# Causal block: rows normalised sequence by sequence, both inverse roots from one variance

## The chip, the cores and the metric

One core of one Trainium2 chip. The time is the device time in microseconds (us) of one launch. Engines in the profile: PE is the tensor engine (TensorE), PEld its weight loads, DVE VectorE, ACT ScalarE, POOL GpSimd, SP the engine that starts DMAs.

## The reference, cut to what matters

The kernel computes a small language-model tower on 8 sequences of 1024 tokens with 64 channels: an embedding from a table, an attention block with 8 heads (called lattice here), and a block with causal attention and a mixture of 8 experts. The change lies in the causal attention. Its input is `h`; it is normalised twice before the projections:

```
x = layernorm(h)                      # (h - mean) / sqrt(var + 1e-5)
def _rmsnorm(v, w): return v * rsqrt(mean(v * v) + 1e-6) * w
h1 = _rmsnorm(x, ln1_w)
q, k, v = h1 @ wq.T, h1 @ wk.T, h1 @ wv.T      # 4 query heads, 2 key/value heads of 16
q = q * cos + rotate_half(q) * sin    # k in the same way
att = softmax(causal(q @ k.T / sqrt(16)))
x = x + (att @ v) @ wo.T
```

The mean square of the layer-normed row follows from the variance alone: with s2 the sum of squares of the centred row and v = s2/64 + 1e-5, the mean of x*x is (s2/64)/v.

## The kernel before

The launch runs four blocks one after the other: `embed`, `lattice`, `causal`, `experts`. All state stays in SBUF: `hres` holds the residual as 128 partitions by 64 rows by 64 channels, `x2` the layer-normed rows. A sequence (called batch, `b`) is 8 of the 64 rows (`TB = 8`), 512 elements on each partition.

`causal` begins with a prologue. GpSimd builds masks, SP loads weights, VectorE folds the norm's weights into them. Then VectorE and ScalarE normalise all 64 rows together (L947 to L968): sum, mean, centring into `x2` (L951), square on ScalarE (L885), sum of squares, variance, root on ScalarE (L887), reciprocal, scaling of `x2` (L960), and a second square, sum, root and reciprocal for the rms norm (`rinv`). Then batch 0 is prepared: `scale_tokens` (L974) makes `xs`, TensorE transposes it (L1046), ScalarE copies it out (L897), TensorE makes the four projections p0 to p3 and the values v (L1058, L1050), VectorE multiplies the projections with the cosine and sine tables (`table`, L984), GpSimd adds their halves and spreads q over the heads (`rope`: L854, L860, and L857 for k), ScalarE copies the values (L901).

The main part runs over batches in `over_batches`: body(0), a hardware loop whose pass holds two batches, then body(7) and a short body(8) that only finishes. A body has 32 units `n`, one for each of 8 blocks of 128 queries and 4 heads; the keys of a unit are 128 to 1024 wide and grow with n (a width for every four units). For unit n:

- TensorE makes the scores (L1084) in one of two score slots, transposes the probabilities of unit n-3 (L1104), and every four units multiplies with the values (L1131) for unit n-5; at n = 6 it applies `wo` (L1112).
- VectorE takes the masked maximum (L1000), copies transposed probabilities (L1014), and takes the reciprocal of the row sum (L1018). Units of VectorE are in this order in its queue.
- ScalarE takes the exponential with its sum (L914) and some of the copies (L924).
- GpSimd multiplies the probabilities with the reciprocal (L871).

The order of everything in a queue is written out by hand. Pieces for batch b+1 stand between the units of batch b: `PIECES` for TensorE (x at 9, p0 to p3 at 13 to 19, v at 21) and `ROPE` for GpSimd (q at 17, heads at 19 to 25, k at 27). At `ADD_AT = 7` VectorE adds the output of the batch before to `x2` (L1022) behind the reciprocal, and GpSimd adds `x2` to `hres` (L877).

`wait` waits on a semaphore, in the instruction that follows. `held`, and a wait with `nop(nofuse=True)` behind it, put the wait into an instruction of its own. In the trace a unit's number is found by counting the maxima (L1000): batch 1's unit 7 starts at 4815.73, unit 28 at 4869.56.

Of the kernel before, what the change touches and what calls it, by code (L numbers as in the profile page):

```python
# [6 lines left out]
ALU = mybir.AluOpType  # L7
ACT = mybir.ActivationFunctionType
AX = mybir.AxisListType.X
# [4 lines left out]
P = 128  # L14
B, S, D = 8, 1024, 64
NT = B * S // P
TB = S // P
# [13 lines left out]
def wait(eng, s, v):  # L31

    if not isinstance(v, int) or v > 0:
        eng.wait_ge(s, v)
# [678 lines left out]
def causal(nc, ident, hres, x2, wqk4, wvT, woT, ln1, cosT, sinT):  # L713

    with ExitStack() as ctx:
        def sb(name, shape, dt=F32):
            return ctx.enter_context(nc.sbuf_tensor(name, shape, dt))
# [1 line left out]
        UNITS = [(qt, h) for qt in range(TB) for h in range(NH)]  # L719
        NU = len(UNITS)  # L720

        sq = sb("c_sq", [P, NT, D])
        s1, mean, s2, var, std, rstd = (sb("c_" + n, [P, NT]) for n in ("s1", "mean", "s2", "var", "std", "rstd"))
        ms, rms, rinv = (sb("c_" + n, [P, NT]) for n in ("ms", "rms", "rinv"))
        lnw = sb("lnw1", [D, 1])
        wqk = sb("c_wqk", [D, 4, P])
        wv = sb("c_wv", [D, NKV * HD])
# [82 lines left out]
        def exists(b):  # L810
            return not isinstance(b, int) or 0 <= b < B

        def over_batches(eng, body):
            body(0, 0)
            with eng.Fori(1, B // 2) as i:
                body(2 * i - 1, 1)
                body(2 * i, 0)
            body(B - 1, (B - 1) % 2)
            body(B, B % 2)

        block = ctx.enter_context(nc.Block())

# [58 lines left out]

        @block.scalar
        def _(act):
            act.wait_ge(ln, 3)
            nc.scalar.activation(sq[:], x2[:], ACT.Square).then_inc(sqd, 1)  # L885
            act.wait_ge(ln, 5)
            nc.scalar.activation(std[:], var[:], ACT.Sqrt).then_inc(rooted, 1)  # L887
            act.wait_ge(ln, 7)
            nc.scalar.activation(sq[:], x2[:], ACT.Square).then_inc(sqd, 1)
            act.wait_ge(ln, 9)  # L890
            nc.scalar.activation(rms[:], ms[:], ACT.Sqrt).then_inc(rooted, 1)

            def tokens_out(b):
                wait(act, xT, b + 1)
# [10 lines left out]
            act.wait_ge(consts, 6)  # L905
            tokens_out(0)
            values_out(0, 0)

            def body(b, par):
                for n in range(steps(b)):  # L910
# [22 lines left out]
                        tokens_out(b + 1)  # L933
                    if pieces(b) and PIECES.get(n) == "v":
                        values_out(b + 1, 1 - par)
            over_batches(act, body)

        @block.vector
        def _(dve):
# [4 lines left out]
            nc.vector.tensor_scalar(wqk[:, 2:4], wqk[:, 2:4], lnw[:, 0:1], None, ALU.mult).then_inc(wmul, 1)  # L944
            nc.vector.tensor_scalar(wv[:], wv[:], lnw[:, 0:1], None, ALU.mult).then_inc(wmul, 1)

            nc.vector.tensor_reduce(s1[:], hres[:], AX, ALU.add).then_inc(ln, 1)  # L947
            dve.wait_ge(ln, 1)
            nc.vector.tensor_scalar(mean[:], s1[:], 1.0 / D, None, ALU.mult).then_inc(ln, 1)
            dve.wait_ge(ln, 2)  # L950
            nc.vector.tensor_tensor(x2[:], hres[:], mean[:].unsqueeze(2).to_broadcast([P, NT, D]),  # L951
                                    ALU.subtract).then_inc(ln, 1)
            dve.wait_ge(sqd, 1)
            nc.vector.tensor_reduce(s2[:], sq[:], AX, ALU.add).then_inc(ln, 1)
            dve.wait_ge(ln, 4)
            nc.vector.tensor_scalar(var[:], s2[:], 1.0 / D, EPS, ALU.mult, ALU.add).then_inc(ln, 1)
            dve.wait_ge(rooted, 1)
            nc.vector.reciprocal(rstd[:], std[:]).then_inc(ln, 1)
            dve.wait_ge(ln, 6)
            nc.vector.tensor_tensor(x2[:], x2[:], rstd[:].unsqueeze(2).to_broadcast([P, NT, D]),  # L960
                                    ALU.mult).then_inc(ln, 1)

            dve.wait_ge(sqd, 2)
            nc.vector.tensor_reduce(s2[:], sq[:], AX, ALU.add).then_inc(ln, 1)
            dve.wait_ge(ln, 8)
            nc.vector.tensor_scalar(ms[:], s2[:], 1.0 / D, EPS_RMS, ALU.mult, ALU.add).then_inc(ln, 1)
            dve.wait_ge(rooted, 2)
            nc.vector.reciprocal(rinv[:], rms[:]).then_inc(ln, 1)  # L968
            dve.wait_ge(ln, 10)

            def scale_tokens(b):

                wait(dve, xT, b)
                nc.vector.tensor_tensor(xs[:], x2[:, bass.ds(b * TB, TB), :],  # L974
                                        rinv[:, bass.ds(b * TB, TB)].unsqueeze(2).to_broadcast([P, TB, D]),
                                        ALU.mult).then_inc(scaled, 1)

            def table(b, par, i):
# [4 lines left out]
                wait(dve, roped, b)  # L983
                nc.vector.tensor_tensor(dst, sc[:, SLOT["p%d" % i]], tab[:], ALU.mult).then_inc(done, 1)  # L984

            scale_tokens(0)
            for i in range(4):
                table(0, 0, i)

            dve.wait_ge(consts, 6)  # L990

            def body(b, par):
                for n in range(steps(b)):
# [22 lines left out]
                    if exists(b):  # L1016
                        wait(dve, expd, NU * b + n + 1)
                        nc.vector.reciprocal(rs[:, par, n:n + 1], sm[:, par, n:n + 1]).then_inc(recip, 1)  # L1018
                    if n == ADD_AT and exists(b - 1):
                        wait(dve, wd, b)  # L1020
                        xv = x2[:, bass.ds((b - 1) * TB, TB), :]
                        nc.vector.tensor_tensor(xv, yp[:].rearrange("p (t d) -> p t d", d=D), xv,  # L1022
                                                ALU.add).then_inc(w_sb, 1)
# [579 lines left out]
```

## Time and profile before

| what | us |
|---|---|
| median of 3 runs (5791.23 to 5793.92) | 5791.73 |
| the profiled execution, its own time | 5820.83 |
| its span | 5819.0 |
| start of the causal prologue's normalising (L947) | 4679.13 |
| first maximum of batch 0 | 4734.01 |
| last addition of the stage (L877) | 5351.86 |

The profiled execution is one of its own and a little longer than the runs that give the median. Times of rows are microseconds from the span's start. The causal stage is about a tenth of the span; `lattice` takes most of the rest, and the change doesn't touch it.

### The profile page before, as it was taken

To read this page: it belongs to the slowest core of one execution; us is meant where nothing else is said; L and a number is where in the kernel's file an instruction comes from. 1 tells how busy PE (TensorE), PEld (TensorE's weight loads), DVE (VectorE), ACT (ScalarE), POOL (GpSimd) and SP (SyncE) were. 2 spreads that over 40 slices of the span, in tenths; PEclk is the share of its full clock that TensorE was granted. 3 is DMA by queue.
4 is the path that set the end of the run, shared out by engine and by line. 5 is a ranking of instruction groups with operands and counts; after the bars stand their busy time and mean duration, and the time that the engine had idled before them with its cause. 6 is when DMAs were issued, how large, how long until landed. Compare 5 with 4: busy or idle time off the path is not lost. (4 is left out here: it accounts for less than half of the span.)

```text
span 5819.0 us, 98405 instructions
## 1 busy us (share of the span) xinstructions
PE 4780.6 (82%) x27646; PEld 2687.0 (46%) x27689; DVE 4160.0 (71%) x7651; ACT 3990.3 (69%) x5494; POOL 3775.7 (65%) x3599
## 2 busy tenths in 40 slices
PE   2788888888888888888888888888888869996999
PEld 1344444444444444444444444444444436554666
DVE  3677777777777777777777777777777656666665
ACT  1677777777777777777777777777777734444332
POOL 4677777777777777777777777777777634443233
PEclk8899999999999999999999999999999879998999
DMA  1000000000000000000000000000000000000000
GB/s 20 9 8 9 8 10 8 8 8 8 8 8 8 8 8 8 9 8 10 8 8 8 8 8 8 8 8 8 9 8 10 3 9 2 2 2 15 3 6 8
DMA packets 34205, 45.42 MB, mean 8 GB/s; under 512 B 24521, under 2 KB 24585, under 8 KB 34058
## 3 DMA queue, kind: packets, MB, share of 16 engines
q1 hardware_dynamic: 32010, 43.49, 2.8%
q0 software_dynamic: 2048, 0.14, 0.1%
q8 instruction: 72, 1.18, 0.1%
q14 instruction: 75, 0.61, 0.0%
HBM read 39.40 MB, written 4.19 MB: 7 GB/s over the span
## 5 line engine op out<-in xcount | busy, mean ns | idle before, releaser
L617 PE MATMUL banks<-ident,att 128*128 128x128 f32 x8192 | 1145.5, 287 | 408.6 <-DVE ag L549 247.1
L617 PEld LDWEIGHTS banks<-ident,att 128*128 128x128 f32 x8192 | 940.7, 147 | 1003.0 <-DVE ag L549 617.4
L659 PE MATMUL banks<-kT,qT 128*128 128x512 f32 x2048 | 1144.1, 658 | 275.8 <-DVE mx L578 266.5
L419 POOL TENSOR_TENSOR sinb<-sinb,ag 128x1024 f32<-128x1024 f32 x512 | 1280.7, 2505 | 82.7 <-ACT sinb L490 68.9
L569 DVE SCALAR_TENSOR_TENSOR mag<-near,mag 128x512 f32<-128x512 int32 x1024 | 859.6, 844 | 479.3 <-POOL near L435 470.6
L429 POOL TENSOR_SCALAR mag<-mag 128x512 f32<-128x512 f32 x1024 | 689.2, 677 | 567.7 <-DVE mag L569 533.7
L676 PE MATMUL outp<-work,vo 128*64 128x512 f32 x2048 | 1043.4, 634 | 0.0
L676 PE MATMUL outp<-sinb,vo 128*64 128x512 f32 x2048 | 1043.4, 634 | 0.0
L435 POOL TENSOR_SCALAR near<-mag 128x512 int32<-128x512 f32 x1024 | 796.4, 778 | 354.2 <-ACT mag L508 291.5
L508 ACT ACTIVATE mag<-banks 128x512 f32<-128x512 f32 x1024 | 598.7, 592 | 278.0 <-PE banks L659 276.4
L526 DVE TENSOR_TENSOR work<-banks,work 128x1024 f32<-128x1024 f32 x512 | 625.3, 1221 | 190.3 <-ACT work L484 187.7
L484 ACT ACTIVATE work<-banks,halfpi 128x1024 f32<-128x1024 f32 x512 | 571.2, 1116 | 239.8 <-PE banks L617 232.8
L490 ACT ACTIVATE sinb<-banks 128x1024 f32<-128x1024 f32 x512 | 522.8, 1021 | 247.7 <-PE banks L633 247.7
L424 POOL TENSOR_SCALAR att<-att,rs 128x1024 f32<-128x1024 f32 x384 | 543.7, 1416 | 214.8 <-DVE rs L543 188.0
L549 DVE TENSOR_TENSOR ag<-banks,work 128x1024 f32<-128x1024 f32 x512 | 621.0, 1213 | 73.3 <-ACT work L513 73.0
L501 ACT ACTIVATE work<-banks 128x1024 f32<-128x1024 f32 x512 | 522.1, 1020 | 155.4 <-PE banks L617 149.0
L659 PEld LDWEIGHTS banks<-kT,qT 128*128 128x128 f32 x2048 | 346.9, 204 | 609.6 <-DVE mx L578 395.1
L472 ACT ACTIVATE att<-att,nb 128x1024 f32<-128x1024 f32 x512 | 582.0, 1139 | 0.8
L513 ACT ACTIVATE work<-work 128x1024 f32<-128x1024 f32 x512 | 541.8, 1058 | 8.3
L676 PEld LDWEIGHTS outp<-work,vo 128*64 128x64 f32 x2048 | 248.0, 141 | 568.9 <-issue 555.6
L578 DVE CUSTOM_DVE_ANT_0 att<-mag,banks 128x512 f32<-128x512 f32 x512 | 348.2, 680 | 211.6 <-POOL mag L429 211.5
L563 DVE TENSOR_SCALAR nturn<-att 128x1024 bf16<-128x1024 f32 x512 | 417.4, 825 | 85.1 <-POOL att L424 85.1
(198 smaller groups left out, 6362.8 us busy)
## 6 DMA issues: line engine op xcount, KB each, us to landing
x<-xT_dram SPq DMA_DIRECT2D x128, 256.0 KB, 3.5
xT_dram<-xT SPq DMA_DIRECT2D x8, 256.0 KB
out<-hres SPq DMA_DIRECT2D x8, 256.0 KB, 2.6
base<-in_L_tok_turns,idx POOLq DMA_INDIRECT x64
wqk<-in_L_attn_Wq SPq DMA_DIRECT2D x64, 16.0 KB
wqk<-in_L_attn_Wk SPq DMA_DIRECT2D x64, 16.0 KB
wqk<-in_L_attn_bq SPq DMA_DIRECT2D x64, 0.2 KB
wqk<-in_L_attn_bk SPq DMA_DIRECT2D x64, 0.2 KB
```

The lines of the kernel that those rows point to most:

```text
L419: nc.gpsimd.tensor_tensor(sinb[:, k % RING], sinb[:, k % RING], ag[:, k], ALU.mult).then_inc(tmul, 1)
L429: nc.gpsimd.tensor_scalar(mag[:, n % 4], mag[:, n % 4], 1.0, PHI, ALU.mult, ALU.add).then_inc(factor, 1)
L435: nc.gpsimd.tensor_scalar(near[:, n % 4], mag[:, n % 4], 1.0 / 6.0, 1.0, ALU.add, ALU.mult).then_inc(rounded, 1)
L472: nc.scalar.activation(att[:, p, j], att[:, p, j], ACT.Exp, bias=nb[:, p, j:j + 1], scale=EXPSCALE, accum_out=ssum[:, j:j + 1]).then_inc(e ...
L484: nc.scalar.activation(pair(work[:, k % RING]), turn_pair(k), ACT.Sin, bias=halfpi[:, 0:1], scale=-C2 / TURN).then_inc(cosd, 1)
L508: nc.scalar.activation(mag[:, n % 4], score_bank(n), ACT.Abs).then_inc(mags, 1)
L526: nc.vector.tensor_tensor(pair(work[:, k % RING]), turn_pair(k), pair(work[:, k % RING]), ALU.mult).then_inc(acd, 1)
L549: nc.vector.tensor_tensor(pair(ag[:, d]), turn_pair(d), pair(work[:, d % RING]), ALU.mult).then_inc(agd, 1)
L569: nc.vector.scalar_tensor_tensor(mag[:, n % 4], near[:, n % 4], 1.0, mag[:, n % 4], ALU.mult, ALU.is_gt).then_inc(kept, 1)
L617: mm = nc.tensor.matmul(turn_pair(k)[:, c, i * P:(i + 1) * P], att[:, p, 4 * half + i, kt * P:(kt + 1) * P], ident[:], is_transpose=True, ...
L659: nc.tensor.matmul(score_bank(n), qT[:, p, (n // 2) * P:(n // 2 + 1) * P], kT[:, p, (n % 2) * 512:(n % 2 + 1) * 512], start=True, stop=Tru ...
L676: mm = nc.tensor.matmul(outp[rows], vo[:, kt, :], term[:, k % RING, c * 512:(c + 1) * 512], start=(kt == 0), stop=(kt == TB - 1), skip_gro ...
```

## The change

Rows are now normalised by sequence. The prologue does the whole chain for batch 0, then batch 1 (its sum and centring before the `table` multiplications of batch 0, the rest behind them). Batch b+2 is normalised between the units of batch b: VectorE does sum and mean after the reciprocal of unit 22, the centring after that of 24, the second moments after 27, the scaling after 30; ScalarE does the square after unit 25 and the root after unit 28. The second mean square is worked out from the first (`rv`, `prod`), so there is one square and one root, over 16 columns, for both norms. Each wait in these parts has a nop of its own. The hardware loop ends one pass earlier, and batches 5 and 6 are written out as 7 and 8 are.

```
--- before.py
+++ after.py
@@ -719,9 +719,10 @@
         UNITS = [(qt, h) for qt in range(TB) for h in range(NH)]
         NU = len(UNITS)
 
-        sq = sb("c_sq", [P, NT, D])
-        s1, mean, s2, var, std, rstd = (sb("c_" + n, [P, NT]) for n in ("s1", "mean", "s2", "var", "std", "rstd"))
-        ms, rms, rinv = (sb("c_" + n, [P, NT]) for n in ("ms", "rms", "rinv"))
+        sq = sb("c_sq", [P, TB, D])
+        s1, mean, s2, rv, prod = (sb("c_" + n, [P, TB]) for n in ("s1", "mean", "s2", "rv", "prod"))
+        moments, root = (sb("c_" + n, [P, 2, TB]) for n in ("moments", "root"))
+        inverse = sb("c_inverse", [P, 2, TB])
         lnw = sb("lnw1", [D, 1])
         wqk = sb("c_wqk", [D, 4, P])
         wv = sb("c_wv", [D, NKV * HD])
@@ -810,13 +811,18 @@
         def exists(b):
             return not isinstance(b, int) or 0 <= b < B
 
+        SUM_AT, CENTRE_AT, SQUARE_AT, MOMENTS_AT, ROOT_AT, SCALE_AT = 22, 24, 25, 27, 28, 30
+
+        def normalised(b):
+            return not isinstance(b, int) or b + 2 < B
+
         def over_batches(eng, body):
             body(0, 0)
-            with eng.Fori(1, B // 2) as i:
+            with eng.Fori(1, B // 2 - 1) as i:
                 body(2 * i - 1, 1)
                 body(2 * i, 0)
-            body(B - 1, (B - 1) % 2)
-            body(B, B % 2)
+            for b in range(B - 3, B + 1):
+                body(b, b % 2)
 
         block = ctx.enter_context(nc.Block())
 
@@ -881,14 +887,18 @@
 
         @block.scalar
         def _(act):
-            act.wait_ge(ln, 3)
-            nc.scalar.activation(sq[:], x2[:], ACT.Square).then_inc(sqd, 1)
-            act.wait_ge(ln, 5)
-            nc.scalar.activation(std[:], var[:], ACT.Sqrt).then_inc(rooted, 1)
-            act.wait_ge(ln, 7)
-            nc.scalar.activation(sq[:], x2[:], ACT.Square).then_inc(sqd, 1)
-            act.wait_ge(ln, 9)
-            nc.scalar.activation(rms[:], ms[:], ACT.Sqrt).then_inc(rooted, 1)
+            def squares(b):
+                wait(act, ln, 10 * b + 3)
+                act.nop(nofuse=True)
+                nc.scalar.activation(sq[:], x2[:, bass.ds(b * TB, TB), :], ACT.Square).then_inc(sqd, 1)
+
+            def roots(b):
+                wait(act, ln, 10 * b + 8)
+                act.nop(nofuse=True)
+                nc.scalar.activation(root[:], moments[:], ACT.Sqrt).then_inc(rooted, 1)
+
+            squares(0)
+            roots(0)
 
             def tokens_out(b):
                 wait(act, xT, b + 1)
@@ -905,6 +915,8 @@
             act.wait_ge(consts, 6)
             tokens_out(0)
             values_out(0, 0)
+            squares(1)
+            roots(1)
 
             def body(b, par):
                 for n in range(steps(b)):
@@ -933,6 +945,10 @@
                         tokens_out(b + 1)
                     if pieces(b) and PIECES.get(n) == "v":
                         values_out(b + 1, 1 - par)
+                    if normalised(b) and n == SQUARE_AT:
+                        squares(b + 2)
+                    if normalised(b) and n == ROOT_AT:
+                        roots(b + 2)
             over_batches(act, body)
 
         @block.vector
@@ -944,35 +960,50 @@
             nc.vector.tensor_scalar(wqk[:, 2:4], wqk[:, 2:4], lnw[:, 0:1], None, ALU.mult).then_inc(wmul, 1)
             nc.vector.tensor_scalar(wv[:], wv[:], lnw[:, 0:1], None, ALU.mult).then_inc(wmul, 1)
 
-            nc.vector.tensor_reduce(s1[:], hres[:], AX, ALU.add).then_inc(ln, 1)
-            dve.wait_ge(ln, 1)
-            nc.vector.tensor_scalar(mean[:], s1[:], 1.0 / D, None, ALU.mult).then_inc(ln, 1)
-            dve.wait_ge(ln, 2)
-            nc.vector.tensor_tensor(x2[:], hres[:], mean[:].unsqueeze(2).to_broadcast([P, NT, D]),
-                                    ALU.subtract).then_inc(ln, 1)
-            dve.wait_ge(sqd, 1)
-            nc.vector.tensor_reduce(s2[:], sq[:], AX, ALU.add).then_inc(ln, 1)
-            dve.wait_ge(ln, 4)
-            nc.vector.tensor_scalar(var[:], s2[:], 1.0 / D, EPS, ALU.mult, ALU.add).then_inc(ln, 1)
-            dve.wait_ge(rooted, 1)
-            nc.vector.reciprocal(rstd[:], std[:]).then_inc(ln, 1)
-            dve.wait_ge(ln, 6)
-            nc.vector.tensor_tensor(x2[:], x2[:], rstd[:].unsqueeze(2).to_broadcast([P, NT, D]),
-                                    ALU.mult).then_inc(ln, 1)
-
-            dve.wait_ge(sqd, 2)
-            nc.vector.tensor_reduce(s2[:], sq[:], AX, ALU.add).then_inc(ln, 1)
-            dve.wait_ge(ln, 8)
-            nc.vector.tensor_scalar(ms[:], s2[:], 1.0 / D, EPS_RMS, ALU.mult, ALU.add).then_inc(ln, 1)
-            dve.wait_ge(rooted, 2)
-            nc.vector.reciprocal(rinv[:], rms[:]).then_inc(ln, 1)
-            dve.wait_ge(ln, 10)
+            def reached(b, k):
+                wait(dve, ln, 10 * b + k)
+                dve.nop(nofuse=True)
+
+            def rows(x, b):
+                return x[:, bass.ds(b * TB, TB), :]
+
+            def wide(x):
+                return x.unsqueeze(2).to_broadcast([P, TB, D])
+
+            def sums(b):
+                nc.vector.tensor_reduce(s1[:], rows(hres, b), AX, ALU.add).then_inc(ln, 1)
+                reached(b, 1)
+                nc.vector.tensor_scalar(mean[:], s1[:], 1.0 / D, None, ALU.mult).then_inc(ln, 1)
+
+            def centre(b):
+                reached(b, 2)
+                nc.vector.tensor_tensor(rows(x2, b), rows(hres, b), wide(mean[:]), ALU.subtract).then_inc(ln, 1)
+
+            def second_moments(b):
+                wait(dve, sqd, b + 1)
+                dve.nop(nofuse=True)
+                nc.vector.tensor_reduce(s2[:], sq[:], AX, ALU.add).then_inc(ln, 1)
+                reached(b, 4)
+                nc.vector.tensor_scalar(moments[:, 0], s2[:], 1.0 / D, EPS, ALU.mult, ALU.add).then_inc(ln, 1)
+                reached(b, 5)
+                nc.vector.reciprocal(rv[:], moments[:, 0]).then_inc(ln, 1)
+                reached(b, 6)
+                nc.vector.tensor_tensor(prod[:], s2[:], rv[:], ALU.mult).then_inc(ln, 1)
+                reached(b, 7)
+                nc.vector.tensor_scalar(moments[:, 1], prod[:], 1.0 / D, EPS_RMS, ALU.mult, ALU.add).then_inc(ln, 1)
+
+            def scale_rows(b):
+                wait(dve, rooted, b + 1)
+                dve.nop(nofuse=True)
+                nc.vector.reciprocal(inverse[:], root[:]).then_inc(ln, 1)
+                reached(b, 9)
+                nc.vector.tensor_tensor(rows(x2, b), rows(x2, b), wide(inverse[:, 0]), ALU.mult).then_inc(ln, 1)
 
             def scale_tokens(b):
 
                 wait(dve, xT, b)
-                nc.vector.tensor_tensor(xs[:], x2[:, bass.ds(b * TB, TB), :],
-                                        rinv[:, bass.ds(b * TB, TB)].unsqueeze(2).to_broadcast([P, TB, D]),
+                reached(b, 10)
+                nc.vector.tensor_tensor(xs[:], rows(x2, b), wide(inverse[:, 1]),
                                         ALU.mult).then_inc(scaled, 1)
 
             def table(b, par, i):
@@ -983,9 +1014,20 @@
                 wait(dve, roped, b)
                 nc.vector.tensor_tensor(dst, sc[:, SLOT["p%d" % i]], tab[:], ALU.mult).then_inc(done, 1)
 
+            def whole(b):
+                sums(b)
+                centre(b)
+                second_moments(b)
+                scale_rows(b)
+
+            whole(0)
             scale_tokens(0)
+            sums(1)
+            centre(1)
             for i in range(4):
                 table(0, 0, i)
+            second_moments(1)
+            scale_rows(1)
 
             dve.wait_ge(consts, 6)
 
@@ -1016,6 +1058,15 @@
                     if exists(b):
                         wait(dve, expd, NU * b + n + 1)
                         nc.vector.reciprocal(rs[:, par, n:n + 1], sm[:, par, n:n + 1]).then_inc(recip, 1)
+                    if normalised(b):
+                        if n == SUM_AT:
+                            sums(b + 2)
+                        if n == CENTRE_AT:
+                            centre(b + 2)
+                        if n == MOMENTS_AT:
+                            second_moments(b + 2)
+                        if n == SCALE_AT:
+                            scale_rows(b + 2)
                     if n == ADD_AT and exists(b - 1):
                         wait(dve, wd, b)
                         xv = x2[:, bass.ds((b - 1) * TB, TB), :]
```

## Rows read from the trace of the kernel before

**Rows 1.** Page, first part: busy us, share of the span, instructions of each engine.
```profile
PE 4780.6 (82%) x27646; PEld 2687.0 (46%) x27689; DVE 4160.0 (71%) x7651; ACT 3990.3 (69%) x5494; POOL 3775.7 (65%) x3599
```

**Rows 2.** Busy times by window: one batch, and the stretch with the low clock.
```profile
4817.00:4895.00 78.00, 73.10 (x584) 47.11 (x584) 51.49 (x136) 36.60 (x84) 34.58 (x40) 0.98 0.01 2
4819.00:4824.00 5.00, 4.26 (x17) 3.11 (x17) 2.37 (x9) 1.85 (x4) 1.37 (x3) 0.66 0.01 3
```

**Rows 3.** Timeline of VectorE, start of the causal stage.
```profile
4679.13 4.41 DVE L947 TENSOR_REDUCE c_s<-hres 128x64 f32<-128x4096 f32 x1
...
4711.12 0.69 DVE L974 TENSOR_TENSOR c_xs<-x,c_rinv 128x512 f32<-128x512 f32 x1
...
4734.01 0.29 DVE L1000 CUSTOM_DVE_ANT_0 c_pr<-c_sc,c_mask 128x128 f32<-128x128 f32 x1 [3.54 <-PE c_sc L1084]
```

**Rows 4.** Timeline of ScalarE, the same stretch.
```profile
4691.89 1.28 ACT L887 ACT_TABLE_LOAD   x1
...
4732.49 0.38 ACT L901 ACTIVATE c_v<-c_sc 128x256 f32<-128x256 f32 x1 [17.43 <-PE c_sc L1050]
```

**Rows 5.** Timeline of VectorE, last batch of the embedding stage.
```profile
125.74 0.69 DVE L189 TENSOR_REDUCE s<-hres 128x8 f32<-128x512 f32 x1
126.46 0.17 DVE L191 TENSOR_SCALAR mean<-s 128x8 f32<-128x8 f32 x1
...
129.69 0.69 DVE L208 TENSOR_TENSOR xn<-cen,rstd 128x512 f32<-128x512 f32 x1
```

**Rows 6.** Timeline of ScalarE, an exponential among the experts.
```profile
5421.45 1.28 ACT L1274 ACT_TABLE_LOAD   x1
5422.74 0.26 ACT L1274 ACTIVATE e_prob<-e_prob 128x64 f32<-128x64 f32 x1
```

**Rows 7.** Timeline of VectorE, units 7 and 8 of batches 0 and 1.
```profile
4741.70 0.42 DVE L1000 CUSTOM_DVE_ANT_0 c_pr<-c_sc,c_mask 128x256 f32<-128x256 f32 x1
...
4742.95 0.56 DVE L1000 CUSTOM_DVE_ANT_0 c_pr<-c_sc,c_mask 128x384 f32<-128x384 f32 x1
...
4815.73 0.42 DVE L1000 CUSTOM_DVE_ANT_0 c_pr<-c_sc,c_mask 128x256 f32<-128x256 f32 x1 [0.21 <-PE c_sc L1084]
...
4817.56 0.55 DVE L1000 CUSTOM_DVE_ANT_0 c_pr<-c_sc,c_mask 128x384 f32<-128x384 f32 x1
...
4818.03 1.72 DVE L974 TENSOR_TENSOR c_xs<-x,c_rinv 128x512 f32 x1
```

**Rows 8.** Timeline of GpSimd: its additions of two tensors, batch 1.
```profile
4817.93 1.27 POOL L877 TENSOR_TENSOR hres<-hres,x  x1 [0.30 <-DVE x L1022]
...
4870.63 2.38 POOL L857 TENSOR_TENSOR c_k<-c_k,c_ks 128x1024 f32<-128x1024 f32 x1
```

**Rows 9.** Timeline, units 25 to 29 of batch 1: VectorE, and TensorE's scores for unit 29.
```profile
4861.89 1.09 DVE L1000 CUSTOM_DVE_ANT_0 c_pr<-c_sc,c_mask 128x896 f32<-128x896 f32 x1 [0.47 <-PE c_sc L1084]
...
4869.33 0.17 DVE L1018 RECIPROCAL c_rs<-c_sm 128x1 f32<-128x1 f32 x1 [0.73 <-ACT c_pr L914]
4869.56 1.22 DVE L1000 CUSTOM_DVE_ANT_0 c_pr<-c_sc,c_mask 128x1024 f32<-128x1024 f32 x1
...
4871.82 1.98 PE L1084 MATMUL c_sc<-c_k,c_qh 128*128 128x512 f32 x4
...
4874.03 1.23 DVE L1000 CUSTOM_DVE_ANT_0 c_pr<-c_sc,c_mask 128x1024 f32<-128x1024 f32 x1 [1.76 <-PE c_sc L1084]
```

**Rows 10.** Timeline of ScalarE, the exponential of unit 29.
```profile
4875.30 1.15 ACT L914 ACTIVATE c_pr<-c_pr,c_nm 128x1024 f32<-128x1024 f32 x1 [2.86 <-DVE c_nm L1000]
```

**Rows 11.** Timeline: unit 1 of batch 2, then units 0 and 1 of batch 3.
```profile
4884.46 0.29 DVE L1000 CUSTOM_DVE_ANT_0 c_pr<-c_sc,c_mask 128x128 f32<-128x128 f32 x1 [0.44 <-PE c_sc L1084]
...
4960.24 0.77 PE L1084 MATMUL c_sc<-c_k,c_qh 128*128 128x128 f32 x2 [3.70 <-issue]
...
4961.35 0.29 DVE L1000 CUSTOM_DVE_ANT_0 c_pr<-c_sc,c_mask 128x128 f32<-128x128 f32 x1 [3.09 <-PE c_sc L1084]
...
4965.38 0.29 DVE L1000 CUSTOM_DVE_ANT_0 c_pr<-c_sc,c_mask 128x128 f32<-128x128 f32 x1 [1.87 <-PE c_sc L1084]
```

## Prediction

> **What bounds the kernel now.** I read the page's first part first: the tensor engine (TensorE) is busy for 82% of the span, VectorE for 71%, ScalarE for 69%, and no DMA queue matters [rows 1]. That says nothing yet of the causal stage, which is a tenth of the span, so I then read the busy times of one of its batches: 78 us with TensorE busy for 73.1, VectorE for 51.5, ScalarE for 36.6 and GpSimd for 34.6 [rows 2]. It looks like a stage that TensorE bounds. The timeline says otherwise. In a unit the order is: VectorE takes the maximum (L1000), ScalarE the exponential (L914), VectorE the reciprocal (L1018), then the next maximum. Maximum and reciprocal sit on one engine with the exponential between them, so a unit can't be shorter than their sum. The reciprocal of unit 27 starts at 4869.33 and the maximum of unit 28 at 4869.56 [rows 9]; nothing else lies between them. TensorE's scores are mostly ready. What VectorE does between a maximum and its reciprocal is hidden behind the exponential; what it does after a reciprocal and ahead of the next maximum is not. The change puts all its new VectorE work in the second place.
>
> A test of this lies in the trace. The addition L1022 (512 columns, as the operations of 0.69 us in [rows 5]) stands after the reciprocal of unit 7, in every batch but the first. Without it the maxima of units 7 and 8 start 1.25 us apart (4741.70, 4742.95), with it 1.83 us (4815.73, 4817.56): 0.58 us of 0.69 comes through [rows 7]. So although TensorE is busy for 94% of the batch, VectorE's work at this place costs nearly its full length.
>
> **The prologue.** All 64 rows are now normalised before any token is scaled: from 4679.13 (L947) to 4711.12 (L974) is 32.0 us, and nothing else runs but these two engines [rows 3]. After the change only eight rows stand there. The embedding stage does almost the same chain on eight rows: from its sum at 125.74 to its scaling at 129.69, 0.69 long, is 4.64 us, each short operation taking 0.17 to 0.2 and starting 0.04 after its predecessor [rows 5]. The new chain has three more short operations (reciprocal of the variance, product, second moment), 3 × 0.21 = 0.6. Its waits are held by a nop of their own. What such a wait costs is seen at unit 29: the scores end at 4871.82 + 1.98 = 4873.80 and the maximum starts at 4874.03, 0.23 later instead of 0.04 [rows 9]. With 11 such links at some 0.17 more, 1.9 us. The table for the root was loaded in the shade of L954 (1.28 us at 4691.89) [rows 4]; now the nop carries the wait and the load stands between nop and root, so I take it as exposed. Bounds: 0 if the load is ahead of the nop, 1.28 if behind; I take 1.28. Sum 4.64 + 0.6 + 1.9 + 1.3 = 8.4, so 23.6 us are saved (bounds 23.6 to 26.8, the latter with neither nops nor load).
>
> Batch 1 is normalised in the prologue too. Its sum and centring fall into VectorE's wait for the first projections, free. Its second half can't: the square stands in ScalarE's queue behind the copy of the values, which starts at 4732.49 and lasts 0.38 [rows 4]. From 4732.9: square 0.6, reduce 0.7, four short operations 0.7, root 0.2, reciprocal 0.2, scale 0.7, and eight links at 0.2 make 4.7, which ends at 4737.6. The first maximum was at 4734.01 [rows 3] and stands behind it: +3.6 us (2.4 with links at 0.04). GpSimd's k rotation, which by the same time runs in batch 0, is over before the product.
>
> **The loop, six batches (b = 0 to 5).** Four blocks on VectorE and two on ScalarE:
> - Sums, after the reciprocal of unit 22: reduce 0.69, link 0.2, mean 0.17, and 0.1 for the register address: 1.2 us.
> - Centring, after unit 24: 0.69 + 0.2 = 0.9. Unit 25's maximum waits 0.47 for TensorE [rows 9], whose order doesn't depend on what was delayed, and that is absorbed: sum so far 1.6.
> - The square on ScalarE after unit 25: about 0.6, in ScalarE's idle time while VectorE takes the next maximum. 0; if that cover were gone, 0.6.
> - Second moments, after unit 27: 0.1 + 0.68, then four short operations of 0.17 to 0.2 and four links of 0.2: 2.3. But the product reads two SBUF tensors, and GpSimd starts its own two-tensor addition L857 at 4870.63, 1.1 us after the reciprocal, for 2.38 us [rows 8]. What happens then is seen in L974: it starts at 4818.03, GpSimd's addition L877 runs from 4817.93 to 4819.20, and the 0.69 us operation takes 1.72 and ends 0.55 after it [rows 7, 8]. So the product is held until L857 ends, 3.5 us after the reciprocal, and the block lasts 3.9. Bounds 2.3 and 3.9, I take 3.9, as the address pattern and the engines are those of the row. Unit 29's maximum waits 1.76 for TensorE [rows 9] and absorbs that much: 2.1 remain.
> - The root, after unit 28's exponential on ScalarE. The table of Exp is resident, so each batch has two loads, root's and back. In the experts stage a load takes 1.28, and the next activation starts 1.29 after the load [rows 6]. Two loads and the root (at most 0.26) are 2.85 with their gaps. ScalarE idled 2.86 ahead of unit 29's exponential [rows 10], but 1.76 of that was TensorE's wait, used up above; 1.1 hide, 1.75 come through. If the moments take 2.3 only, some 1.2 come through.
> - Scaling, after unit 30: 0.1 + reciprocal 0.2 + link 0.3 + 0.69 = 1.3, no two-tensor GpSimd work beside it.
>
> A batch costs 1.6 + 2.1 + 1.75 + 1.3 = 6.75 us, six cost 40.5. Without the hold on the product it is 1.6 + 0.5 + 1.2 + 1.3 = 4.6, six 27.6.
>
> The Trainium skill's page ScalarE: Activation LUTs (What ACT_TABLE_LOAD costs) has 1283 ns for the load and about 1380 ns of drain, 2.66 us a switch. The load agrees; the drain isn't in the rows. By the page, 12 switches would cost 12 × 1.37 = 16.4 us more.
>
> **The loop's edge.** The change also unrolls two batches more, so the loop is passed twice instead of three times and turns back once instead of twice. A turn costs: TensorE sits 3.70 for issue, VectorE idles 3.09 ahead of unit 0 and 1.87 ahead of unit 1, where 0.44 is usual [rows 11]. One turn less is −4.5 us. Unrolled batches have constants for registers; I take nothing for that (at most 1 us in all). The nop ahead of each scaling of tokens (seven) adds about 0.1 each behind no cover: +0.7, and SP issues nothing new.
>
> **Sum.** −23.6 + 3.6 + 40.5 − 4.5 + 0.7 = +16.7 us. The profiled execution took 5820.83, its span 5819.0; it would take 5837.5. The runs' median lies 29 below the profiled time, and no part of this is in the causal stage that I can see, so I add to the median: 5791.7 + 16.7 = 5808.4.
>
> **The rivals.** Changes within 0.2%, 11.6 us, are what a measurement of this kernel can't tell from none.
> - *The product isn't held (chance 0.2).* An eight-column operation may slip between the other engine's reads; no row shows so small a one beside L857. For it: TensorE is idle for only 5 us of 78, so a delay is soaked up more easily than I let it. Then −23.6 + 3.6 + 27.6 − 4.5 + 0.7 = +3.8: 5795.5.
> - *Faster (0.13): TensorE is the bound after all.* 94% busy speaks for it, unit 7 against. TensorE would catch up a delay of units 22 to 31 in the narrow units 0 to 8 of the next batch, where VectorE waits for it again and again. Then each batch gives back all but 2 us: −23.8 + 12 = −12: 5779.9. It decides below 2.1 us a batch.
> - *TensorE's clock (0.17).* At 4819 to 4824 the granted clock was 0.66 of full, a mixture of 2.4 and 1.2 GHz, after TensorE had idled for about a microsecond, and its matmuls were slower [rows 2]. It happened in one batch of six at that place. Idle stretches of some 4 us at units 28 to 30 could bring it in every batch: I take 2 us each, from the 1.87 − 0.44 = 1.4 that follows the loop's turn and up. +12: 5820.4.
> - *The table switch costs its drain (0.05)*: 1.37 us exposed twelve times, as worked out above: 5825.
> - My own case has the rest, 0.45, with 5802 to 5813.
>
> **Numbers.** 5808.4; range 5784 to 5824, which leaves out most of the faster case and the end of the dearest. Faster by over 0.2% (below 5780.1): 0.1. Within it: the first rival, half of the faster one and a sixth of mine: 0.34. Slower (above 5803.3): 0.56.
>
> **What the profile after would show.** L974's first instruction some 8.4 us after the first sum, not 32. The first maximum of batch 0 3.6 us later behind the projections than now. Product's duration about 1.8 us and not 0.17 in each of the six batches, ending as L857 ends. Two loads of 1.28 a batch around the root, and the exponential of unit 29 late by them. Six batches longer by some 6.8 us from unit 22 to the next unit 0. One idle stretch of 3.7 us of TensorE for issue in place of two. I am wrong if TensorE's idle time doesn't grow by what VectorE's does, if units 0 to 8 get shorter after a late unit 31, or if the load comes ahead of the nop.

## The result

| | before | changed |
|---|---|---|
| median of 13 runs each, us | 5791.88 | 5814.66 |
| ratio, 95% interval | | 1.0035 [1.0026, 1.0043] |
| span of the profiled execution, us | 5819.0 | 5810.4 |
| start of attention's last addition (L538) to the first maximum, us | 63.7 | 41.5 |
| first to last maximum, us | 605.3 | 649.3 |
| the whole stage, from that start to the start of the last addition to `x2`, us | 680.7 | 702.5 |

The change makes the kernel slower by 0.35%, some 20 us (15 to 25). The two spans seem to say the opposite, but the profiled execution of before had lost time ahead of the stage: its attention block starts (L398) at 136.7 and that of the changed kernel at 105.8. Inside the causal stage the traces differ by 702.5 − 680.7 = 21.8 us, which fits the measured 20. I therefore compare stages, not spans, from here on. In the changed kernel VectorE's maximum is L1042, its reciprocal L1060, the exponential L926, the scores L1135, GpSimd's multiplication L877 and its k rotation L863.

The prologue of the changed kernel, VectorE (answers to [rows 3]):

```profile
4649.67 0.67 DVE L974 TENSOR_REDUCE c_s<-hres 128x8 f32<-128x512 f32 x1
4650.44 0.17 DVE L976 TENSOR_SCALAR c_mean<-c_s 128x8 f32<-128x8 f32 x1
...
4656.90 0.69 DVE L1006 TENSOR_TENSOR c_xs<-x,c_inverse 128x512 f32<-128x512 f32 x1
...
4679.27 0.69 DVE L985 TENSOR_REDUCE c_s<-c_sq 128x8 f32<-128x512 f32 x1 [3.03 <-ACT c_sq L893]
...
4682.46 0.28 DVE L1042 CUSTOM_DVE_ANT_0 c_pr<-c_sc,c_mask 128x128 f32<-128x128 f32 x1
```

and ScalarE in the same stretch (to [rows 4]):

```profile
4654.13 1.28 ACT L898 ACT_TABLE_LOAD   x1 [2.00 <-DVE c_moments L993]
...
4678.26 0.38 ACT L911 ACTIVATE c_v<-c_sc 128x256 f32<-128x256 f32 x1 [17.42 <-PE c_sc L1101]
4678.54 0.62 ACT L893 ACTIVATE c_sq<-x 128x512 f32<-128x512 f32 x1
```

From the first sum to the scaling of tokens it is 7.2 us instead of 32.0. The load stands behind the wait for the moments, exposed. From there to the first maximum it is 25.6 instead of 22.9, because batch 1's second half waits for a square that stands behind the copy of the values.

Units 27 to 31 of batch 1 in the changed kernel, VectorE (to [rows 9]):

```profile
4827.70 0.16 DVE L1060 RECIPROCAL c_rs<-c_sm 128x1 f32<-128x1 f32 x1 [0.73 <-ACT c_pr L926]
4827.87 0.69 DVE L985 TENSOR_REDUCE c_s<-c_sq 128x8 f32<-128x512 f32 x1
4828.66 0.41 DVE L987 TENSOR_SCALAR c_moments<-c_s 128x8 f32<-128x8 f32 x1
4829.17 0.20 DVE L989 RECIPROCAL c_rv<-c_moments 128x8 f32<-128x8 f32 x1
4829.48 1.92 DVE L991 TENSOR_TENSOR c_prod<-c_s,c_rv 128x8 f32<-128x8 f32 x1
4831.50 0.17 DVE L993 TENSOR_SCALAR c_moments<-c_prod 128x8 f32<-128x8 f32 x1
4831.75 1.22 DVE L1042 CUSTOM_DVE_ANT_0 c_pr<-c_sc,c_mask 128x1024 f32<-128x1024 f32 x1
...
4834.58 1.22 DVE L1042 CUSTOM_DVE_ANT_0 c_pr<-c_sc,c_mask 128x1024 f32<-128x1024 f32 x1
...
4841.52 0.16 DVE L1060 RECIPROCAL c_rs<-c_sm 128x1 f32<-128x1 f32 x1 [0.84 <-ACT c_pr L926]
4841.60 0.25 DVE L998 RECIPROCAL c_inverse<-c_root 128x16 f32<-128x16 f32 x1
4841.96 1.55 DVE L1000 TENSOR_TENSOR x<-x,c_inverse 128x512 f32 x1
4843.43 1.21 DVE L1042 CUSTOM_DVE_ANT_0 c_pr<-c_sc,c_mask 128x1024 f32<-128x1024 f32 x1
...
4846.26 0.29 DVE L1042 CUSTOM_DVE_ANT_0 c_pr<-c_sc,c_mask 128x128 f32<-128x128 f32 x1
...
4849.90 0.29 DVE L1042 CUSTOM_DVE_ANT_0 c_pr<-c_sc,c_mask 128x128 f32<-128x128 f32 x1 [2.06 <-PE c_sc L1135]
```

GpSimd beside it (to [rows 8]):

```profile
4829.01 2.36 POOL L863 TENSOR_TENSOR c_k<-c_k,c_ks 128x1024 f32<-128x1024 f32 x1
...
4841.85 1.12 POOL L877 TENSOR_SCALAR c_pr<-c_pr,c_rs 128x1024 f32<-128x1024 f32 x1 [1.66 <-DVE c_rs L1060]
```

ScalarE at unit 29 (to [rows 6, 10]):

```profile
4834.65 1.28 ACT L898 ACT_TABLE_LOAD   x1
4835.94 0.22 ACT L898 ACTIVATE c_root<-c_moments 128x16 f32<-128x16 f32 x1
4836.17 1.28 ACT L926 ACT_TABLE_LOAD   x1
4837.47 1.15 ACT L926 ACTIVATE c_pr<-c_pr,c_nm 128x1024 f32<-128x1024 f32 x1
```

and two groups of TensorE's transposes, between the scores of unit 31 and those of unit 0 of batch 2:

```profile
4838.64 0.60 PE L1155 MATMUL c_pt<-ident,c_pr 128*128 128x128 f32 x4
4842.11 1.09 PE L1155 MATMUL c_pt<-ident,c_pr 128*128 128x128 f32 x4 [2.88 <-ACT c_prT L936]
```

The product of eight columns takes 1.92 us and ends with GpSimd's addition (4829.01 + 2.36 = 4831.37). The wide scaling takes 1.55 and ends 0.54 after GpSimd's L877, which has one tensor only. Two loads and a root stand in a row ahead of the exponential. TensorE then waits 2.88 us for a copy, and its next four transposes take 1.09 where four took 0.60.

The granted clock in the 6 us from unit 0 of batch 2, the changed kernel (busy times of the engines, then the clock, as in [rows 2]):

```profile
4846.00:4852.00 6.00, 5.90 (x81) 4.98 (x80) 3.37 (x13) 2.25 (x8) 1.86 (x3) 0.76 0.02 4
```

and the kernel before at the same place:

```profile
4882.00:4888.00 6.00, 5.86 (x108) 5.02 (x110) 4.37 (x18) 3.62 (x13) 2.24 (x4) 1.00 0.02 4
```

In the kernel before the clock is 1.00 at the start of batches 1, 2, 4 and 6, and 0.79 at that of 3 and 5, where the loop has just turned. In the changed kernel it is 0.65 to 0.82 at the start of all six. Such a window catches only the end of the slow stretch: ahead of batch 2 of the changed kernel the clock is 0.50 from 4842, as TensorE comes out of its wait of 2.88 us, to 4849, and unit 0 starts at 4846.26. Unit 31 lies in this stretch and costs nothing more (2.83 us, 2.85 before); unit 0 does.

Laid side by side by the starts of the maxima, batch 1 (unit 0: the start of batch 2), us from one unit's maximum to the next:

| unit | 22 | 24 | 27 | 28 | 29 | 30 | 0 |
|---|---|---|---|---|---|---|---|
| before | 2.36 | 2.93 | 2.54 | 4.47 | 2.78 | 2.78 | 2.02 |
| changed | 3.68 | 3.16 | 6.35 | 2.83 | 4.40 | 4.45 | 3.64 |
| difference | +1.3 | +0.2 | +3.8 | −1.6 | +1.6 | +1.7 | +1.6 |

Over all batches the 44.0 us between first and last maximum are: units 22 to 30 +39.3, unit 0 +5.9, unit 9 +3.2, unit 31 −3.4 (the loop's turn), the rest −1.0.

### The profile page after: what moved, and what is told of

It reads as the page before. It is cut to its first block and busy times, and to the rows that moved or that the text cites. A ratio compares the mean times of both kernels' runs of the same rounds, so it can differ in the third digit from the quotient of the medians.

```text
span 5810.4 us, 98228 instructions
## 1 busy us (share of the span) xinstructions
PE 4804.7 (83%) x27689; PEld 2704.4 (47%) x27689; DVE 4185.2 (72%) x7721; ACT 4004.3 (69%) x5518; POOL 3777.1 (65%) x3599
```

## The experiments

They ran on other chips, on which the kernel before took 5855 to 5860 us (medians) and scattered more; the ratio is always to runs of before on the same chip. An effect of 10 us (0.17%) doesn't show in such times, but it does in the stage of one trace, whose units 22 to 30 repeat from run to run within some 0.02 us where nothing was done to them. Units 0 and 9 don't: the clock decides their length, and they carry up to 3 us from one trace to another.

**Move GpSimd's k rotation.**

```
-        ROPE = {17: "q", 19: 0, 21: 1, 23: 2, 25: 3, 27: "k"}
+        ROPE = {17: "q", 19: 0, 21: 1, 23: 2, 25: 3, 28: "k"}
```

> The changed kernel with one number changed: GpSimd's k rotation stands behind unit 28 instead of 27, so it no longer runs beside the second moments. Theory (the product of eight columns is held by the two-tensor addition, 1.6 us a batch): the product takes 0.17 us in the loop instead of 1.91, the interval from the maximum of unit 27 to that of 28 falls from 6.35 to about 4.7, the sum of the causal stage (first to last maximum, 649.3 us) falls by 6 x 1.6 = 10, the time is some 10 us below the changed kernel's 5812. Rival (TensorE sets the pace there, or the operation is slow for another reason): the product gets short and unit 28 or 29 gives the time back, or it stays at 1.9; the sum stays at 649.

Ratio 1.0006 [0.9959, 1.0052]: the time says nothing. The stage is 690.8 us, 11.7 less than the changed kernel's 702.5. The interval of unit 27 fell from 6.35 to 4.60, that of 29 stayed at 4.39 and 30 at 4.45. The product for batch 2, worked out in batch 0:

```profile
4786.38 0.17 DVE L991 TENSOR_TENSOR c_prod<-c_s,c_rv 128x8 f32<-128x8 f32 x1
```

So the product was held by that one addition, 1.75 us a batch (10.4 of the 11.7; the rest is unit 9's), and nothing gives it back. One of its batches also shows that the slow stretch moves about: ahead of batch 3, where the loop turns, TensorE waits 2.79 us as ahead of batch 2, the clock is 0.50 from 4965 to 4972, and unit 0, which starts at 4972.09, takes 1.84 us at 1.00.

**No table switch in the loop.** A copy replaces the root of batches 2 to 7, so the root is left out there.

```
+                func = ACT.Sqrt if isinstance(b, int) and b < 2 else ACT.Copy
-                nc.scalar.activation(root[:], moments[:], ACT.Sqrt).then_inc(rooted, 1)
+                nc.scalar.activation(root[:], moments[:], func).then_inc(rooted, 1)
```

> The changed kernel with a copy in place of the root in batches 2 to 7, so that ScalarE keeps its table (what is computed is no longer the normalisation there). Theory (two table loads of 1.28 us, 1.6 us of them exposed at unit 29): the interval from the maximum of unit 29 to that of 30 falls from 4.40 to about 2.8, the stage by 6 x 1.6 = 10 us or more, since TensorE also idles less and its clock may stay up at the next unit 0. Rival (the page's 2.66 us for each switch): 4.3 us a batch, 26 in all. Second rival (TensorE's or GpSimd's lateness lies behind the loads): less than 3 us in all.

Ratio 1.0008 [0.9963, 1.0052]. The stage is 692.3 us, 10.3 less. Unit 29 fell from 4.40 to 2.78 and no other unit between 22 and 30 moved. Two switches a batch cost 1.62 us, not the rival's 4.3; but unit 0 stayed at about 3.6, so the clock was not won back.

**Both edits** (the root is left out here too).

> Both edits of the two runs before together: the k rotation behind unit 28 and no table switch in the loop. The question is the granted clock at the start of the next batch. In the changed kernel it is 0.65 to 0.82 in the 6 us from unit 0, where the kernel before has 1.00 unless the loop has just turned, and the interval from unit 0 to unit 1 is 1.4 to 2.0 us longer. Theory (the clock falls because TensorE has idled at units 28 to 31): with both stalls gone the clock is 1.00 there, unit 0 back at 2.0 us, and the two together save more than the sum of the two alone: 2 x 10 + 6 x 1.6 = 30 us, about 5783. Rival (unit 0 is late because TensorE has work left over, or the fall comes from elsewhere): the savings just add, 20 us, about 5792.

Ratio 1.001 [0.9964, 1.0057], stage 685.2: 17.3 less, not 30 and not even the 22 that the two add up to. Units 27, 29 are at 4.60 and 2.78. But unit 0 is no better: 3.49 to 4.28 us in five batches of six (2.88 behind the loop's turn). The window from unit 0 of batch 2, columns as before:

```profile
4916.00:4922.00 6.00, 5.98 (x68) 5.10 (x69) 2.05 (x8) 2.03 (x8) 1.50 (x2) 0.50 0.01 3
```

My expectation failed: the clock is 0.50, that is 1.2 GHz, for the whole window. It didn't fall lower than in the changed kernel, but later. Here the 0.50 lasts from 4915 to 4922, and unit 0 starts at 4916.88, so most of it falls on units 0 and 1. What was left was the stall behind unit 30. TensorE's transposes ahead of unit 0 came behind a wait of 1.96 us:

```profile
4916.02 1.09 PE L1156 MATMUL c_pt<-ident,c_pr 128*128 128x128 f32 x4 [1.96 <-DVE c_prT L1057]
```

**Both edits, and the scaling ahead of unit 30's reciprocal.**

```
+                    if normalised(b) and n == SCALE_AT:
+                        scale_rows(b + 2)
                     if exists(b):
                         wait(dve, expd, NU * b + n + 1)
                         nc.vector.reciprocal(rs[:, par, n:n + 1], ...)
...
-                        if n == SCALE_AT:
-                            scale_rows(b + 2)
```

> The run with both edits (k rotation behind unit 28, no table switch) and the scaling of unit 30 put ahead of the reciprocal. With both edits TensorE's clock still fell at the next unit 0 (3.5 to 4.3 us from unit 0 to 1, 2.0 in the kernel before); what was left there was the scaling, 1.7 us between units 30 and 31. Theory (that stall is what the clock falls after): unit 30's interval about 3.3 or less, unit 0's back at 2.0, clock 1.00 in the 6 us from unit 0. Rival (the stall at unit 27, or something of the units 28 to 31 as a whole): unit 0 stays at 3.5 or more.

One execution, 5827.6 us, so there is no ratio; the stage is 663.0, 22.2 less than with both edits alone. Unit 30 is at 2.78 as in the kernel before: the scaling has vanished under the exponential. Unit 0 is at 1.87 to 2.17, but for the loop's turn (3.75). The same window, and the same transposes:

```profile
4886.00:4892.00 6.00, 5.90 (x102) 5.03 (x104) 4.28 (x17) 3.70 (x13) 2.25 (x4) 1.00 0.02 4
```

```profile
4885.83 0.63 PE L1156 MATMUL c_pt<-ident,c_pr 128*128 128x128 f32 x4 [0.30 <-DVE c_prT L1057]
```

So with the other two gone, one stall of 1.7 us at unit 30 cost 22.2 / 6 = 3.7 us a batch: itself (10.2 of the 22.2 are unit 30's), and about as much again in slow matmuls (10.9 in units 0 and 1, 1.0 in unit 9).

**The scaling alone moved ahead**, held product and table loads in place; the diff is the one above, made to the changed kernel.

> The changed kernel with the scaling of unit 30 alone put ahead of the reciprocal; the held product and the table loads stay. Theory (TensorE's clock falls at unit 0 behind the scaling's stall, whatever came before): unit 30's interval 4.45 to 2.8 and unit 0's 3.2 to 4.0 back to about 2.0, 3.5 us a batch, the stage 702.5 to about 681. Rival (the clock falls after the sum of stalls from unit 27 on, so that with product and tables still there it falls anyway): unit 0 stays at 3.5, the stage at 692.

Ratio 1.0008 [0.9989, 1.0027], stage 688.5, 14.0 less. Of these 10.2 are unit 30's, and 3.0 unit 9's, which was slow in one batch instead of three for a reason that isn't known; without these 3.0 the stage would be at 691.5, near the rival's figure. Unit 30 is at 2.78, unit 0 at 2.9 to 3.4 outside the loop's turn, which is 0.9 to 1.4 above what it was before, and 5.04 behind the turn (4.03 before). The theory failed: the fall isn't tied to the scaling alone. TensorE's wait of 2.88 us at unit 30 is still there, and the fall comes behind it. This wait belongs to the table loads: it is 2.79 us with the rotation moved and 1.2 without the loads. Unit 0 does get shorter outside the turn (3.9, 3.6, 3.4, 4.0 and 3.5 were 3.1, 3.0, 2.9, 3.0 and 3.4).

**All four blocks ahead of the reciprocals.**

```
                     if exists(b):
-                        wait(dve, expd, NU * b + n + 1)
-                        nc.vector.reciprocal(...)                      # unit n
                     if normalised(b):
                         if n == SUM_AT:
                             sums(b + 2)
...
+                    if exists(b):
+                        wait(dve, expd, NU * b + n + 1)
+                        nc.vector.reciprocal(...)
```

> The changed kernel with VectorE's four blocks ahead of the reciprocals of units 22, 24, 27 and 30 instead of behind them, where they run while ScalarE takes the exponential. Theory (a unit is maximum, exponential, reciprocal in series, so only the place behind the reciprocal costs its full length): most of the blocks is covered, 0.5 to 0.9 us each; the product is also done before GpSimd's k rotation starts, since that waits for this reciprocal. The intervals fall at 22 from 3.68 to about 3.1, at 27 from 6.35 to about 3.6, at 30 from 4.45 to about 3.3; unit 29 stays at 4.4 (the tables). The sum from first to last maximum falls from 649.3 to some 625. Rival (VectorE's total or TensorE bounds the units, the place makes no odds): it stays within 3 us of 649.

Ratio 0.9967 [0.995, 0.9983]: faster than before. The stage is 660.4 us, 42.1 less than the changed kernel's, and the sum between first and last maximum 606.8; I had expected 625. Units 22 and 27 are at 2.97 and 3.41, 24 at 2.93, 28 at 3.60 (up from 2.83), 29 at 3.63, 30 at 2.78, and unit 0 at 1.87 to 2.19 but for the loop's turn. TensorE's longest wait at units 27 to 31, the turn aside, is 1.6 us, and its clock stays at 1.00. The moments of batch 2, VectorE:

```profile
4783.22 0.17 DVE L991 TENSOR_TENSOR c_prod<-c_s,c_rv 128x8 f32<-128x8 f32 x1
4783.49 0.17 DVE L993 TENSOR_SCALAR c_moments<-c_prod 128x8 f32<-128x8 f32 x1
4783.57 0.15 DVE L1069 RECIPROCAL c_rs<-c_sm 128x1 f32<-128x1 f32 x1
```

GpSimd's k rotation starts at 4784.87 there, after the product: in GpSimd's queue it stands behind L877, which waits for this reciprocal. My expectation was 18 us too small. The clock, which I had left out, makes 7.7 of them at unit 0; unit 30 gave 3.3 more than expected, because the scaling was covered in full, units 22, 24 and 27 gave 1 each, and unit 9 1.6. Against the kernel before, units 22 to 30 are 6.5 us a batch longer in one place, with a slow start of the next batch, and 1.0 us in the other.

**The loop alone.**

```
-            with eng.Fori(1, B // 2) as i:
+            with eng.Fori(1, B // 2 - 1) as i:
                 body(2 * i - 1, 1)
                 body(2 * i, 0)
-            body(B - 1, (B - 1) % 2)
-            body(B, B % 2)
+            for b in range(B - 3, B + 1):
+                body(b, b % 2)
```

> The kernel before with only the loop changed: one pass fewer, batches 5 and 6 written out. Theory (a turn of the loop costs 3.7 us of issue on TensorE and a fallen clock behind it, 4.95 us by the maxima of units 31 and 0): 5 us less, 5787, the stage 605.3 to about 600. Rival (written-out batches cost instruction fetches of their own): no change or slower.

Ratio 0.9982 [0.9933, 1.0031], which can't tell 5 us from none; stage 675.4, 5.3 less. One stretch of units 31 and 0 went from 5.9 + 3.9 to 2.9 + 2.0.

**Both roots from one variance, alone**: as in the changed kernel, but over all 64 rows in the prologue of the kernel before.

> The kernel before with one part of the change alone: all 64 rows still normalised in the prologue, but both roots from one variance (one square, one sum of squares and one root fewer, three short operations more). Theory: a square of 3.6 us and a reduction of 4.4 go, some 1 us comes; the first maximum is 8 us earlier (63.7 to about 55.7 us from the end of the attention block), everything behind it as before: 8 us less. Rival: nothing, because the projections or the weights are what the prologue waits for; the first maximum stays at 63.7.

Ratio 0.9988 [0.9972, 1.0004], which takes in both 7 us and none. In the trace the first maximum comes at 56.6 us instead of 63.7 (counted as in the table above), where 55.7 was expected, and from first to last maximum it is 605.1 as before: 7.1 us less. This half of the change was good.

**The rows in the gaps of the prologue.** The other seven batches, in pieces of 24 and 32 rows:

```
+            sums(0)
+            centre(0)
+            second_moments(0)
+            scale_rows(0)
             dve.wait_ge(w_in, 144)
...
             scale_tokens(0)
+            sums(1)
+            centre(1)
+            sums(2)
             table(0, 0, 0)
+            centre(2)
             table(0, 0, 1)
+            second_moments(1)
             table(0, 0, 2)
+            second_moments(2)
             table(0, 0, 3)
+            scale_rows(1)
+            scale_rows(2)
```

> A version built on the theory: batch 0 is normalised while VectorE waits for the weights (7.4 us idle in the kernel before), the other seven batches in two pieces in the gaps of VectorE between the projections of batch 0, nothing in the units; loop one pass shorter. Theory (the prologue's gaps are free, the units' are not): first maximum 63.7 - 32 + 3 to 6 = 35 to 38 us after the end of the attention block, the sum from first to last maximum 599.8 as with the short loop alone, the whole stage 680.7 to about 649, some 32 us (0.55%) faster than before. Rival (the pieces are held by GpSimd's rotation or push the projections back): first maximum at 45 or later, 20 us or less.

Ratio 0.9944 [0.9923, 0.9965]. First maximum at 38.9, a little later than expected, from first to last 598.2, stage 648.8, 31.9 less than before. VectorE in the gaps:

```profile
4701.05 0.35 DVE L988 TENSOR_SCALAR c_wqk<-c_wqk,lnw 64x256 f32<-64x256 f32 x1 [1.05 <-DMA c_wo<-in_woT]
...
4718.08 1.07 DVE L972 TENSOR_SCALAR c_moments<-c_prod 128x24 f32<-128x24 f32 x1
...
4725.02 3.71 DVE L980 TENSOR_TENSOR x<-x,c_inverse 128x1536 f32<-128x1536 f32 x1
...
4729.23 2.29 DVE L980 TENSOR_TENSOR x<-x,c_inverse 128x2048 f32<-128x2048 f32 x1
```

and GpSimd:

```profile
4716.90 4.41 POOL L862 TENSOR_SCALAR c_qh<-c_q,c_own 128x1024 f32<-128x1024 f32 x4 [0.18 <-POOL c_q L856]
4724.78 2.34 POOL L859 TENSOR_TENSOR c_k<-c_k,c_ks 128x1024 f32<-128x1024 f32 x1 [3.48 <-DVE c_ks L1008]
```

The weights are now waited for 1.05 us instead of 7.4. The row of the kernel before:

```profile
4678.45 0.34 DVE L942 TENSOR_SCALAR c_wqk<-c_wqk,lnw 64x256 f32<-64x256 f32 x1 [7.41 <-DMA c_wo<-in_woT]
```

The scaling of 24 rows is held by the k rotation (3.71 us, fewer elements than the 2.29 us behind it).

**The same, all batches written out, no loop.**

```
+            for b in range(B + 1):
+                body(b, b % 2)
```

> The version with the pieces in the projections' gaps, and all batches written out, no loop. Theory (a turn of the loop costs 4.9 us, written-out instructions are fetched in time): the interval from unit 31 of batch 2 to unit 0 falls from 5.81 to about 3.0 and the next from 4.21 to 2.2, the stage 648.8 to about 643, 38 us (0.65%) faster than before. Rival (instruction fetches fall behind when nothing is looped): stalls for issue on TensorE at other places, the stage at 649 or above.

Ratio 0.9921 [0.9896, 0.9946], the fastest version run. Stage 640.4, 40.3 less than before and 8.4 less than with the loop: 5.2 in units 31 and 0, the rest spread over the other units of the batches that had been in the loop. The batches between the first and the last last 75.1 us each, where those of the loop took 76 to 79, and the clock at unit 0 is 1.00 in all of them. No wait of TensorE for issue replaces the loop's turn.

## Why the prediction was right

The time, 5791.9 × 1.0035 = 5812, lies 4 above the forecast of 5808.4 (the median of the 13 runs 6 above), in the range and on the side foreseen. The mechanism was mine; several terms were off, and one rival was true as well. That the sum came so near is partly luck: it left out up to 11.1 us of lower clock, and 4.8 us of terms that were too dear stood against them.

- *Prologue*: −23.6 was forecast, 32.0 − 7.2 = 24.8 saved. The load is exposed as supposed; a held wait costs about 0.10 here (4649.67 + 0.67 to 4650.44), not 0.2, so the saving was put too small. For the same reason batch 1's delay was 2.7, not 3.6.
- *Work behind a reciprocal comes through in full*: right, and shown by moving it. Units 22 to 30 gave 39.3 us against 40.5 forecast.
- *The held product*: 3.9 us forecast for the block at unit 27, 3.8 measured; shown by the moved rotation.
- *The table loads*: 1.75 forecast, 1.62 measured; the drain of the Trainium skill's page ScalarE: Activation LUTs (What ACT_TABLE_LOAD costs) isn't there: the root starts 1.29 us after its load's start, and the Exp load's successor 1.30 after.
- *The absorbed waits of TensorE*: at unit 29's maximum 1.76 forecast, 1.64 measured; at unit 25's, 0.47 forecast: unit 24's interval grew by 0.2, where 0.9 − 0.47 would be 0.4.
- *Scaling*: "no two-tensor GpSimd work beside it" named the wrong condition. L877, with one tensor, holds it too: 1.7 instead of 1.3. What [rows 7, 8] showed was one scaling beside one two-tensor addition, and I took the kind of GpSimd's operation for the cause. What counts in the traces is which of the two began first (see the last section).
- *The loop's edge*: −4.5 forecast, −5.3 measured alone.
- *The nops of the token scaling*: +0.7 forecast, nothing measured (unit 8: 2.17 before and after).
- *The clock*: a rival with 0.17, priced at 2 us a batch and thought of as an alternative. It came on top. Unit 0 of six batches takes 21.6 us in all; with the loop alone shortened it takes 13.7. So it costs 7.9 us, 1.3 a batch, and two slow units 9 more than before another 3.2. That the stall at unit 30 brings it is shown by the run in which it disappears; that it also comes without the stall at unit 30, by the run with the scaling alone moved. What settles when the slow stretch begins, and so how much of it unit 0 bears, stays open. The slow unit 9 comes in from none to three batches of a trace, also in the kernel before and in versions without any stall at units 27 to 30, always with the clock low (0.54 to 0.58 in it); why in these batches stays open, and whether the 3.2 belong to the change at all.

With the clock's 7.9 + 3.2 in place of nothing, the 0.7 struck out, and the prologue 1.2 + 0.9 better, my 16.7 becomes 16.7 + 11.1 − 0.7 − 2.1 − 1.2 − 0.8 = 23.0, with 39.3 for 40.5 and 5.3 for 4.5; the traces say 21.8. Of the 1.2 between them 0.7 is unit 9 again, slower by that in the run with the loop alone, so that its 5.3 is too small a saving; the rest I can't place.

## What to carry to other kernels

When two engines work in series within a unit, ask of each added operation on which side of the other engine's turn it stands: the same four blocks cost 42 us more behind the reciprocal than ahead of it, though TensorE was 94% busy. A busy share of 94% is no proof that the engine sets the pace, and here a late engine that made it idle for 2 to 3 us was paid twice, the second time in matmuls at the lower clock (1.3 us a batch in the changed kernel, 2.0 with both edits). Before work is spread into a tuned loop, look for the gaps of the prologue: there all of it cost some 7 us (first maximum at 38.9 us, where 63.7 − 32.0 = 31.7 would be none).

## What the runs showed of the hardware

- A VectorE operation that begins while GpSimd works on SBUF can be held until GpSimd's ends. The product of eight columns with two SBUF tensors, begun 0.47 us after L863, took 1.92 us for 0.17 of work; the scaling of 512 columns, begun 0.11 us after L877, took 1.55 for 0.69 and ended 0.54 us after L877, which has one tensor. VectorE's operation need not have two either: the 8-column L987 took 0.41 beside L877 and ended within 0.03 us of it (4829.07, L877 from 4828.03 for 1.01), and a 24-column one 1.07. But the reciprocal of eight columns at 4829.17, 0.20 long, ran unhindered within L863. The GpSimd row of L877 in that place is:

```profile
4828.03 1.01 POOL L877 TENSOR_SCALAR c_pr<-c_pr,c_rs 128x896 f32<-128x896 f32 x1 [1.52 <-DVE c_rs L1060]
```

- The one that began first wasn't lengthened in these rows. At unit 24 the centring, with two SBUF tensors, began 0.09 us ahead of L877 and took its 0.69; here it was GpSimd's operation that took 1.49 us instead of 1.01, in this batch and (1.32 to 1.49) in the other five:

```profile
4819.67 0.69 DVE L980 TENSOR_TENSOR x<-hres,c_mean 128x512 f32 x1
4819.76 1.49 POOL L877 TENSOR_SCALAR c_pr<-c_pr,c_rs 128x896 f32<-128x896 f32 x1 [0.54 <-DVE c_rs L1060]
```

- The Trainium skill's GPSIMD Engine Reference (1. Specifications) says that the interfaces to SBUF are shared with VectorE and that VectorE's operations contend with GpSimd's where they have two SBUF inputs or run in a mode that uses both ports; this row of it sets no condition on GpSimd's. The product and the scaling agree (1.92 and 1.55 us), and by that rule contention would have been expected at the scaling too.
- A loop's turn makes TensorE wait 3.0 to 3.9 us for issue in these traces; in the kernel before unit 0 behind it takes 3.9 to 4.0 us instead of 2.0, at a clock of 0.79. Written out, the stage was 5.3 us shorter for one turn less: 3.0 in unit 31 and 1.9 in unit 0. Nine batches written out had no such cost anywhere.
